# A residual block of two 3x3 convolutions: another order of the first two steps on all engines

## The reference

```
def _bn(x, gamma, beta, mean, var):
    inv = gamma * jax.lax.rsqrt(var + EPS)
    return x * inv[None, :, None, None] + (beta - mean * inv)[None, :, None, None]

out = relu(_bn(conv3x3(x, w1), g1, b1, m1, v1))
out = _bn(conv3x3(out, w2), g2, b2, m2, v2)
return relu(out + x)
```

## Time and profile before

| | us |
|---|---|
| median of 3 runs | 580.67 |
| the profiled execution, as timed | 580.64 |
| its span (first to last instruction) | 579.0 |
| TensorE busy | 567.1 (98%) |
| VectorE busy | 546.2 (94%) |
| ScalarE busy | 493.1 (85%) |
| GpSimd busy | 37.2 (6%) |

### The profile page before, as it was taken

The page is one execution under the profiler, slowest core; times in us unless marked ns, Lnnn a source line. Parts: engine busy times, 40 slices in busy tenths (PEclk is TensorE's granted clock), DMA queues, the critical chain, the costliest instruction groups (busy, mean ns, idle before and its releaser), DMA issues.

```text
span 579.0 us, 9009 instructions
## 1 busy us (share of the span) xinstructions
PE 567.1 (98%) x3058; PEld 543.4 (94%) x3058; DVE 546.2 (94%) x462; ACT 493.1 (85%) x744; POOL 37.2 (6%) x44
## 2 busy tenths in 40 slices
PE   7889999999999999999999999999999999999997
PEld 4569999999999999999999999999999999999997
DVE  6799999999999999999999999999999999999985
ACT  3488888998888998888998888998888998888985
POOL 6200000000000000000000000000000000000000
PEclk9899999999999999999999999999999999999999
DMA  8733455544445544455544455544455544451112
GB/s 263 199 103 110 132 144 149 165 146 121 130 143 150 163 145 120 131 143 150 163 145 115 137 143 152 162 140 129 127 143 150 163 150 122 128 144 46 39 57 111
DMA packets 31407, 79.20 MB, mean 137 GB/s; under 512 B 2592, under 2 KB 19104, under 8 KB 31392
## 3 DMA queue, kind: packets, MB, share of 16 engines
q1 hardware_dynamic: 26784, 66.05, 31.5%
q0 software_dynamic: 4464, 12.89, 14.5%
q10 hardware_dynamic: 144, 0.07, 0.1%
HBM read 53.31 MB, written 25.69 MB: 136 GB/s over the span
## 4 chain that ended last, share of the span: by engine, by line
PE 93%; DVE 3%; ACT 2%; issue 1%; DMA 1%; ACTq 0%
PE psum L664 93%; DMA bn<-params_dram 1%; DVE x_lo L384 1%; ACT x_hi L515 1%; DVE psum L398 1%; DVE w_lo L198 0%; DVE t_outer L358 0%; DVE x_inner L369 0%; ACT hidden L555 0%; ACT psum L525 0%; ACT w_hi L193 0%; DVE t_inner L414 0%; DVE x_inner L354 0%; DVE x_inner L352 0%; DVE inv L337 0%
## 5 line engine op out<-in xcount | busy, mean ns | idle before, releaser
L664 PE MATMUL psum<-x_hi,w_hi 128*128 128x420 f32 x496 | 172.3, 347 | 0.5 <-DVE w_lo L198 0.5
L664 PE MATMUL psum<-x_hi,w_lo 128*128 128x420 f32 x496 | 168.8, 340 | 0.0
L664 PE MATMUL psum<-x_lo,w_hi 128*128 128x420 f32 x496 | 168.5, 340 | 0.0
L398 DVE TENSOR_TENSOR psum<-psum,z 128x784 f32<-128x784 f32 (+1 forms) x128 | 127.1, 993 | 3.6 <-ACT hidden L555 1.6
L664 PEld LDWEIGHTS psum<-x_hi,w_hi 128*128 128x128 f32 x496 | 93.1, 188 | 6.4 <-issue 4.0
L664 PEld LDWEIGHTS psum<-x_hi,w_lo 128*128 128x128 f32 x496 | 93.2, 188 | 0.8
L664 PEld LDWEIGHTS psum<-x_lo,w_hi 128*128 128x128 f32 x496 | 93.2, 188 | 0.5
L555 ACT ACTIVATE hidden<-psum,bias,half_inv 64x56 f32<-64x56 f32 (+2 forms) x128 | 84.5, 687 | 5.9 <-PE psum L664 4.7
L664 PE MATMUL psum<-h_hi,w_hi 128*128 128x392 f32 x256 | 87.3, 341 | 0.0
L664 PE MATMUL psum<-h_hi,w_lo 128*128 128x392 f32 x256 | 87.2, 341 | 0.0
L664 PE MATMUL psum<-h_lo,w_hi 128*128 128x392 f32 x256 | 87.1, 340 | 0.0
(11 more groups left out here) (62 smaller groups left out, 809.6 us busy)
## 6 DMA issues: line engine op xcount, KB each, us to landing
x_sb<-x_dram SPq DMA_DIRECT2D x32, 814.0 KB, 4.8
out_dram<-out_sb SPq DMA_DIRECT2D x63, 392.0 KB, 2.8
x_inner<-x_dram SPq DMA_DIRECT2D x31, 406.0 KB, 3.2
x_inner<-x_dram POOLq DMA_DIRECT2D x31, 406.0 KB, 5.0
out_dram<-out_sb SPq DMA_DIRECT2D x2, 196.0 KB, 2.3
z<-w_dram SPq DMA_DIRECT2D x1, 384.0 KB, 3.7
out_sb<-w_dram SPq DMA_DIRECT2D x1, 384.0 KB, 6.3
bn<-params_dram ACTq DMA_DIRECT2D x1, 68.0 KB, 3.9
```

Of the source, the lines that this page charges most:

```text
L398: nc.vector.tensor_tensor(psum[:, half, EVEN:ODD + 1, 0:width], t1, z[:, half, :, 0:width], ALU.add).then_inc(joined[conv], 1)
L664: ins = nc.tensor.matmul(sums, w[:, i, far, :], t[:, j0:j1, 0:WQ], start=not onto and at == 0, stop=at == len(todo) - 1, skip_group_check= ...
```

## The change

All of it lies in steps 0 and 1 and ahead of them, and in the counts of a few semaphores later on.

- GpSimd zeroes the first 420 columns of `hidden` by themselves (TensorE's warm-up waits for these) and the rest after that; it issues image 1's accumulation ahead of the norm; it does no work on the second filters.
- VectorE transforms the first filters first, then the norm's `var`, then image 0's x, then the rest of the norm. In step 0: join, difference of image 1, join, low half of the first filters, split of image 1's inner planes, its outer planes, scaling of the second filters. In step 1: outer planes of hidden 0, join, transform of the second filters, join, sum and difference of hidden 0, difference of image 2, split of hidden's outer planes, outer planes and inner split of image 2, join of the second convolution, low half of the second filters, outer split of image 2.
- Image 1's outer planes are not split: TensorE multiplies them in native fp32.
- ScalarE makes the outer filters ahead of the square root; both ReLUs of image 0 come at the end of step 0; in step 1 the second filters' high half comes behind the first ReLU of image 1.
- TensorE in step 1: image 1's inner products, then its outer products, then image 0's inner products of the second convolution, each for both halves, then the wait for the second filters' low half.

```diff
+        def split_of_x(which, n):
+            return n - 1 if which == "outer" else n
...
         @block.gpsimd
-            nc.gpsimd.memset(hidden[:], 0.0).then_inc(zeroed, 1)
+            nc.gpsimd.memset(hidden[:, 0:MAXN], 0.0).then_inc(zeroed, 1)
+            nc.gpsimd.memset(hidden[:, MAXN:], 0.0).then_inc(zeroed, 1)
...
+            add_odd(1, 1)
             after = chain(pool, bn_step)
...
-            add_odd(1, 1)
-
-            pool.wait_ge(w_in[2], 16)
-            pool.wait_ge(bn_step, 2)
-            part = w_raw[2].rearrange("p k f (s c) -> p (k f) s c", c=C)
-            scale = half_inv[:, 2:].unsqueeze(1).unsqueeze(1).broadcast_to((P, 6, 2, C))
-            pool.tensor_tensor(part, part, scale, ALU.mult).then_inc(w2_scaled, 1)
-
-            pool.wait_ge(w2_scaled, 1)
-            double_inner_filters(pool, 2, chain(pool, prep[2]))
...
         @block.vector
+            def norm():
+                after = chain(dve, newton)
+                dve.wait_ge(std_ready, 1)
+                nc.vector.reciprocal(inv[:], inv[:]).then_inc(recip_ready, 1)
+                dve.wait_ge(recip_ready, 1)
+                after(nc.vector.tensor_tensor(tmp[:], inv[:], inv[:], ALU.mult))
+                after(nc.vector.tensor_tensor(tmp[:], tmp[:], var[:], ALU.mult))
+                after(nc.vector.tensor_scalar(tmp[:], tmp[:], -0.5, 1.5, ALU.mult, ALU.add))
+                after(nc.vector.tensor_tensor(inv[:], inv[:], tmp[:], ALU.mult))
+
+            def scale_filters_2():
+                dve.wait_ge(w_in[2], 16)
+                dve.wait_ge(bn_step, 2)
+                part = w_raw[2].rearrange("p k f (s c) -> p (k f) s c", c=C)
+                scale = half_inv[:, 2:].unsqueeze(1).unsqueeze(1).broadcast_to((P, 6, 2, C))
+                nc.vector.tensor_tensor(part, part, scale, ALU.mult).then_inc(w2_scaled, 1)
...
+            dve.wait_ge(w_in[1], 16)
+            double_inner_filters(dve, 1, chain(dve, prep[1]))
+            dve.wait_ge(bn_in, 16)
+            nc.vector.tensor_scalar(var[:], bn[:, 0:COLS], EPS, None, ALU.add).then_inc(var_ready, 1)
             first_x()
-            low_weights(dve, 1)
+            norm()
...
             def outer_x(n, k):
-                wait(dve, xlo_ready["outer"], n - 1)
+                if is_step(n, 2):
+                    dve.wait_ge(outer[1], 4)
+                wait(dve, xlo_ready["outer"], n - 2)
...
                 if is_step(s, 0):
+                    join(1, 0, 0, (2, -2))
                     difference_x(1, 1)
-                    join(1, 0, 0, (2, -2))
+                    join(1, 0, 1, (2, -2))
+                    low_weights(dve, 1)
+                    split_x("inner", 1, 1)
                     outer_x(1, 1)
-                    join(1, 0, 1, (2, -2))
-                    split_x("inner", 1, 1)
-                    split_x("outer", 1, 1)
+                    scale_filters_2()
+                    return
+                if is_step(s, 1):
+                    outer_hidden(0)
+                    join(1, 1, 0, (2, -1))
+                    dve.wait_ge(w2_scaled, 1)
+                    double_inner_filters(dve, 2, chain(dve, prep[2]))
+                    join(1, 1, 1, (2, -1))
+                    sum_hidden(0)
+                    difference_hidden(0)
+                    difference_x(2, 2)
+                    split_hidden("outer", 0, 0)
+                    outer_x(2, 2)
+                    split_x("inner", 2, 2)
+                    join(2, 0, 0, before_conv2(0))
+                    low_weights(dve, 2)
+                    split_x("outer", 2, 2)
                     return
...
         @block.scalar
+            act.wait_ge(w_in[1], 16)
+            double_outer_filters(1)
             act.wait_ge(var_ready, 1)
             nc.scalar.activation(inv[:], var[:], ACT.Sqrt).then_inc(std_ready, 1)
-
-            act.wait_ge(w_in[1], 16)
-            double_outer_filters(1)
             high_weights(1)
...
+                if is_step(s, 0):
+                    copy_sum(1, 0, 0)
+                    copy_sum(1, 0, 1)
+                    high_x("inner", 1, 1)
+                    act.wait_ge(bias_ready, 1)
+                    act.wait_ge(zeroed, 2)
+                    relu_hidden(0, 0)
+                    relu_hidden(0, 1)
+                    return
+                if is_step(s, 1):
+                    copy_sum(1, 1, 0)
+                    copy_sum(1, 1, 1)
+                    high_hidden("outer", 0, 0)
+                    residual(0, 0, 0)
+                    act.wait_ge(w2_scaled, 1)
+                    double_outer_filters(2)
+                    residual(0, 0, 1)
+                    high_x("inner", 2, 2)
+                    relu_hidden(1, 0)
+                    high_weights(2)
+                    copy_sum(2, 0, 0)
+                    high_x("outer", 2, 2)
+                    copy_sum(2, 0, 1)
+                    return
...
         @block.tensor
-            def whole_passes(conv, i):
+            def whole_passes(conv, i, image=0):
...
+                if image:
+                    return ((x_outer[:, OUTER[1][i]].rearrange("p (j c) -> p j c", c=WQ + 1), wmat[1]),)
...
+                if is_step(s, 1):
+                    pe.wait_ge(xlo_ready["inner"], 1)
+                    for half in range(2):
+                        for i, bank in ((2, SUM_T2), (1, SUM_T1)):
+                            sum_products(1, half, i, bank, passes_of(1, i, 1), False).then_inc(inner[1], 1)
+                    pe.wait_ge(tx_ready["outer"], 2)
+                    for half in range(2):
+                        outer_products(1, 1, 1, half)
+                    pe.wait_ge(prep[2], 3)
+                    for half in range(2):
+                        inner_products_2(0, half)
+                    pe.wait_ge(wlo_ready[2], 1)
+                    return
```

More of the change, by code:

```diff
@@ L381, in split_x @@
                 full, places = x_full(which, k)
-                dve.wait_ge(xhi_ready[which], n)
+                dve.wait_ge(xhi_ready[which], split_of_x(which, n))
                 nc.vector.tensor_tensor(x_part(x_lo, k, places), full,
@@ L419, in outer_hidden @@
                 rows = hidden_rows(half)
+                if is_step(n, 0):
+                    dve.wait_ge(hidden_ready, 2)
                 wait(dve, hlo_ready["outer"], n)
@@ L467, in step @@
                     difference_hidden(s - 1)
-                if last and not is_step(s, 1):
+                if last:
                     split_hidden("t1", s - 1, kl % 2)
@@ L489, in step @@
                     join(2, s - 1, 0, before_conv2(s - 1))
-                if is_step(s, 1):
-                    low_weights(dve, 2)
                 if ahead:
@@ L562, in relu_hidden @@
                 wait(act, th_ready["outer"], n)
+                if is_step(n, 1):
+                    act.wait_ge(th_ready["t1"], 1)
+                    act.wait_ge(th_ready["t2"], 1)
                 src = psum[:, half, EVEN:ODD + 1, 0:(k1 - k0) * WQ].rearrange("p s (r q) -> p s r q", q=WQ)
@@ L622, in step @@
                     copy_sum(1, s, 1)
[L623 to L626, removed]
                 if there_is(s, s - 2):
@@ L634, in step @@
                     high_x("inner", s + 1, ka)
-                if is_step(s, 0):
-                    act.wait_ge(bias_ready, 1)
-                    act.wait_ge(zeroed, 1)
                 if now:
@@ L708, in outer_products @@
                 for i, bank in ((0, EVEN), (3, ODD)):
-                    passes = whole_passes(1, i) if conv == 1 and is_step(n, 0) else passes_of(conv, i, b)
+                    first = conv == 1 and (is_step(n, 0) or is_step(n, 1))
+                    passes = whole_passes(1, i, n) if first else passes_of(conv, i, b)
                     ins = sum_products(conv, half, i, bank, passes, True)
@@ L762, in step @@
                         outer_products(2, s - 2, k % 2, half)
-                if is_step(s, 1):
-                    pe.wait_ge(prep[2], 3)
                 for half in range(2):
@@ L769, in step @@
                     if now:
-                        pe.wait_ge(xlo_ready["outer"], s)
+                        pe.wait_ge(xlo_ready["outer"], s - 1)
                         outer_products(1, s, k % 2, half)
-                if is_step(s, 1):
-                    pe.wait_ge(wlo_ready[2], 1)
             run(pe, step)
```

## The result

The changed kernel takes 574.07 us (median of four, 573.88 to 574.53) where the kernel before took 580.61: a ratio of 0.9892, interval 0.9879 to 0.9906. The profiled execution took 574.53 us, with a span of 572.9. Forecast were 574.8 and faster.

What follows compares the result with a forecast made beforehand. TensorE was taken to bound the kernel from step 2 on, other engines before it. Step 2 starting at 36.05 instead of 41.91 saves 5.86: 580.64 - 5.86 = 574.8 us, bounds 573.8 to 575.8, 8-in-10 range 573.3 to 577.2.

Steps and rivals of the forecast that it cites:

- The bound: From step 2 on TensorE is the limit; the gain is how much earlier step 2's first matmul starts, 5.86 us.
- The first image: Ahead of step 2: image 0's x starts at 6.53, 1.57 us earlier; TensorE is through image 0 at 18.65, not 24.69.
- The half clock: TensorE's products behind the 2.8 us wait ran partly at 1.2 GHz; without that wait their extra 1.66 us go.
- Rival (a): The clock falls in a new TensorE wait ahead of step 2, in some executions only: 576.5, both places 577.3; chance 0.16.
- The landing: Image 1's accumulating DMA of odd rows, issued at 7.6, lands at 15.0, between 13.0 and 16.0.
- The chain: VectorE runs without a wait from image 1's inner split at 16.55 through the second low weights: 19.15 us, to 35.7.
- The thinnest cover: Before join(2, 0, 0), ScalarE's copies end at 33.4 and VectorE arrives at 33.6: 0.2 us to spare.
- The native products: Image 1's outer products in native fp32 cost TensorE 1.25 us more, hidden in its 1.35 us wait before step 2.
- (b): VectorE isn't the limit ahead of step 2; TensorE's own work decides, step 2 at about 34.7, 573.4 us; chance 0.06.
- (c): Something other than TensorE paces the steps, so the earlier start is given back as a later wait: 580.6; chance 0.05.
- (d): Steady steps begin out of phase and TensorE waits each turn; slower from 0.20 us a step, 583.8 at 0.3; chance 0.05.

Runs made afterwards that it cites:

- the two kernels with one part alone: Kernel before with only the second filters' work moved to VectorE: 577.07 us; kernel before with only the new order of the first 15 us: 576.99 us.
- first experiment: Changed kernel with image 1's outer planes split again into high and low halves, 24 matmuls instead of 16 native records: 577.22 us, 0.9946.
- the control: Changed kernel with two loads moved later on SP's queue, one warm-up product less, and steps 2 to 5 written out: 573.08 us.

## Why the prediction was right

**The bound.** That the time follows step 2's start held in both profiled executions (6.14 and 6.11). It holds as long as VectorE and ScalarE come as much earlier as TensorE does; the kernel with the outer difference moved shows the limit of that reading: TensorE's 1.4 us wait is not a reserve, since the step behind it is only just fed.

**The first image.** The times came out within 0.3 us: filters from 4.47 (4.6 forecast), x from 6.49 (6.53), first products at 7.62 (7.65), the first join at 11.59 (11.7), image 0 through TensorE at 18.39 (18.65). The choice of 1.76 for t_outer, against the bound of 3.47, rested on GpSimd's work beside it; the two kernels with one part alone show that this was the right reason, since either way of taking that work away gives 1.78.

**The half clock.** The 1.66 us that the sum let go with the 2.8 us wait were there in the profiled execution before (580.64 us, mean granted clock 0.997), but not in each. Of the 40 executions of the kernel before that ran beside the experiments, 26 have a mean clock of 0.994 to 0.997 and took 579.9 to 582.0 us, and 14 have 1.00 and took 578.9 to 579.6; the changed kernel's eight have 0.999 or 1.00. So against an execution at full clock, about 579.2, the change is worth 5.1 us, not 6.5; the sum was made against one with the stretch. None of the 40 was traced, so the stretch in them is inferred from the mean. Rival (a) had said of the new waits that the same pause may cost in some executions only, and this fits it.

**The landing.** 15.0 was forecast, 14.78 measured, but the reasoning was only half right. The DMA packets by queue in two stretches of the changed kernel, 9 to 10 us and 11.5 to 12.5 us (queue, kind: packets, MB, share):

```profile
q1 hardware_dynamic: 93, 0.39, 96.0%
...
q0 software_dynamic: 60, 0.19, 105.6%
```

From 9 to 10 us, more than a microsecond behind the accumulation's issue, only SP's loads (q1) move; from 11.5 to 12.5, with two further SP loads issued at 10.08 and 10.46, only the accumulation (q0). So over these stretches the two queues did not share, they went one after the other. That the accumulation waited for the loads issued ahead of it is shown by moving them: its first packets come at about 10.5 us here, at 9.5 with the loads moved later (SP's last ones were through by 9.2) and at 11.8 or later with one load more, though it was issued at 7.7 to 7.8 each time. Issuing it 1.3 us earlier brought nothing by itself (14.78 against 14.50 before). The Trainium skill (DMA: Bandwidth & Descriptors, section "Queues, rings and completion order") has the engines take packets in turn from the queues that have work; here both queues move packets only where one takes over from the other, from 10.5 to 11.5 us (25 of the accumulation's beside 46 of SP's) and from 12.9 to 13.5 (31 beside 24), with five last ones of the accumulation's among 94 of SP's after that. The landing differs by execution, 13.8 to 14.8 in the traces with this order of loads, and below 13.9 it is VectorE itself that sets the split. In the two traces of the changed kernel this mis-sized term is most of what the forecast had too late: 0.22 of 0.28 us (step 2 at 35.77 instead of 36.05) and 0.59 of 0.65 (35.40). That it also makes the 0.7 us of the median fits this, but the other executions were not traced.

**The chain.** From the start of the split to the end of the second low weights 19.15 us were summed; it was 35.45 - 16.35 = 19.10, without idle time. The thinnest cover held: ScalarE's copies ended at 32.87, VectorE came at 33.34.

**The native products.** They took 5.51 and lay in the wait, as forecast; that TensorE was left with 1.37 us (1.35 forecast) was not their only use. Without them (first experiment) the waits grew to 1.8 and 2.4 and the clock fell. Together with the shorter VectorE chain they are worth 3.0 to 3.2 us; of that the forecast had counted the split (1.78) alone, not the 1.7 of the half clock.

**Rivals.** (a) did not come here; it came in the first experiment, and by its mean clock in one execution of the control; (b), (c) and (d) did not come: behind step 2's start TensorE has no wait, and the time from there to the end is the same. What the forecast did not price: a second load of ScalarE's function table, 1.28 us at 5.21 ahead of the square root. It held the square root up to 6.51 (var was there at 5.80), which cost nothing: VectorE took the norm up at 9.97.

## What to carry to other kernels

Find the point from which the bounding engine never waits again, and sum the other engines' chain up to it from start to start: here that came within 0.05 us in 19. A helper engine that works beside the busy one can double its instructions, so the place of helper work decides more than its length; and two edits that each look worth 3.5 us may in part remove the same stall. Look at the mean clock of each execution before calling its scatter noise. A last wait of the bounding engine is a gain only if what feeds the next steps moves with it.

## What the hardware showed that was not expected

- VectorE's long instructions with both inputs in SBUF took 2.23 to 2.38 us beside GpSimd's tensor instructions instead of 1.78 to 1.84, and in two cases 3.04 and 3.47. Its joins, with one input in PSUM, kept their 0.97 to 1.03 beside them, and beside GpSimd's DMA issue t_outer kept its 1.78.
- An accumulating DMA and SP's loads went one behind the other in the order of issue, for 1 us or more at a time; both moved packets only around the change from one to the other.
- By the mean granted clock the stretch at half clock came in 26 of 40 executions of one and the same kernel, which took 1.4 us more than the other 14.
- At the loop's entry the first matmul came 0.33 us behind its release (0.50 in one trace), in straight code 0.04; steps in the loop took 17.37 us on the average, written out 17.33.
